# A third gathered tree, normalised rows and row sums kept in PSUM, and new orders in a fused attention and tree feed-forward kernel

## The reference

```python
x = x + attn(layernorm(x)); x = x + ffn(layernorm(x))
# attn: query, keys, values = unit_projection(x @ W.T + b)   f = fft(y); y = ifft(f/(|f|+1e-8)).real
#       s = cumsum(bind(keys, values), axis=1); out = unbind(s, query)        (products of spectra)
# ffn:  8 trees of depth 7 with 255 nodes each. logits = x @ W_in.T + b_in; decisions = logits > 0
#       a token walks from the root of each tree to one leaf; acts = silu(logits) count only on the path
#       out = masked_acts @ W_out.T
```

## Time and profile before

| | us |
|---|---|
| median of 3 runs (1918.32 to 1920.07) | 1919.68 |
| profiled execution, device time | 1920.69 |
| its span, first to last instruction | 1918.9 |
| TensorE busy in it | 1867.1 |
| VectorE busy | 1500.1 |
| ScalarE busy | 1118.4 |
| GpSimd busy | 946.1 |

### The profile page before, as it was taken

The page is one execution under the profiler, slowest core; times in us unless marked ns, Lnnn a source line. Parts: engine busy times, 40 slices in busy tenths (PEclk is TensorE's granted clock), DMA queues, the critical chain, the costliest instruction groups (busy, mean ns, idle before and its releaser), DMA issues.

```text
span 1918.9 us, 40326 instructions
## 1 busy us (share of the span) xinstructions
PE 1867.1 (97%) x14680; PEld 1417.2 (74%) x14680; DVE 1500.1 (78%) x2874; ACT 1118.4 (58%) x2151; POOL 946.1 (49%) x736
## 2 busy tenths in 40 slices
PE   8599999999999999999999999999999999999978
PEld 6478777778777778877777877777877777887755
DVE  4878778877877877877877877787787787788783
ACT  5666565566555566556556656556656555655643
POOL 1254445564454565444555444556444556545450
PEclk9799999999999999999999999999999999999998
DMA  8022232222133222223222223222213322222212
GB/s 285 12 78 81 74 99 88 77 88 87 55 99 99 66 88 88 67 86 99 77 84 86 82 66 99 93 71 88 88 56 97 99 75 79 88 67 87 88 56 66
DMA packets 181784, 163.18 MB, mean 85 GB/s; under 512 B 140160, under 2 KB 140800, under 8 KB 181760
## 3 DMA queue, kind: packets, MB, share of 16 engines
q1 hardware_dynamic: 163328, 95.48, 16.8%
q0 software_dynamic: 18432, 67.38, 10.6%
HBM read 95.72 MB, written 16.78 MB: 59 GB/s over the span
## 4 chain that ended last, share of the span: by engine, by line
PE 93%; DVE 1%; DMA 0%; SPq 0%; ACT 0%; issue 0%; DVEq 0%; ACTq 0%
PE bank_l L531 31%; PE bank_l L591 30%; PE bank_p L481 24%; PE bank_l L541 3%; PE bank_i L481 2%; PE bank_i L552 1%; PE bank_i L561 0%; PE bank_i L562 0%; PE bank_i L560 0%; PE bank_i L559 0%; DMA arena<-xn_pair 0%; PE bank_i L558 0%; PE bank_i L571 0%; SPq L340 0%; DVE xn_pair L1127 0%
## 5 line engine op out<-in xcount | busy, mean ns | idle before, releaser
L531 PE MATMUL bank_l<-arena,win_mem 128*128 128x256 f16 x5376 | 626.1, 273 | 14.4 <-DMA arena<-xn_pair 14.4
L591 PE MATMUL bank_l<-wout_mem,arena 128*128 128x512 f16 x2688 | 590.6, 379 | 0.0
L531 PEld LDWEIGHTS bank_l<-arena,win_mem 128*128 128x128 f16 x5376 | 527.3, 99 | 76.5 <-DMA arena<-xn_pair 14.2
L481 PE MATMUL bank_p<-arena,wf_hi 128*128 128x256 f16 x3072 | 506.3, 273 | 2.7 <-ACT arena L742 2.7
L591 PEld LDWEIGHTS bank_l<-wout_mem,arena 128*128 128x128 f16 x2688 | 263.1, 98 | 303.4 <-DVE arena L1224 0.2
L481 PE MATMUL bank_p<-arena,wf_lo 128*128 128x256 f16 x1536 | 419.3, 273 | 0.0
L986 POOL TENSOR_TENSOR arena<-arena 128x512 f32<-128x512 f32 x96 | 121.7, 1268 | 570.2 <-ACT arena L751 570.2
L481 PEld LDWEIGHTS bank_p<-arena,wf_hi 128*128 128x128 f16 x3072 | 299.8, 98 | 37.7 <-ACT arena L742 3.0
L796 ACT ACTIVATE arena<-bank_l,bias_in,s_logit 128x256 f32<-128x256 f32 x448 | 229.6, 556 | 142.1 <-PE bank_l L541 141.6
L1224 DVE SCALAR_TENSOR_TENSOR arena<-arena,s_act 128x512 f16<-128x512 f32 (+1 forms) x256 | 195.5, 765 | 133.7 <-ACT arena L806 131.2
L1217 DVE TENSOR_SCALAR dec<-bank_l,thr,off 128x256 bf16<-128x256 f32 x256 | 135.8, 541 | 91.5 <-PE bank_l L531 88.8
(11 more groups left out here) (178 smaller groups left out, 2490.3 us busy)
## 6 DMA issues: line engine op xcount, KB each, us to landing
arena<-in_x SPq DMA_DIRECT2D x32, 512.0 KB, 3.5
arena<-arena SPq DMA_DIRECT2D x32, 512.0 KB, 2.9
out<-arena SPq DMA_DIRECT2D x64, 256.0 KB, 2.1
wout_mem<-in_w_in_t SPq DMA_DIRECT2D x1, 3584.0 KB, 15.4
arena<-in_w_out_t SPq DMA_DIRECT2D x1, 3584.0 KB, 14.2
arena<-xn_pair SPq DMA_TRANSPOSE x128, 2.7
arena<-in_leaf_rows,leaf_row POOLq DMA_INDIRECT x128, 5.5
win_mem<-in_wq SPq DMA_DIRECT2D x1, 1024.0 KB, 8.2
```

The lines of the kernel that those rows point to most:

```text
L481: mm = pe.matmul(bank, a, b, start=(n == 0), stop=(n == len(pairs) - 1))
L531: mm = pe.matmul(bank_l[t % 4][:, c * T:(c + 1) * T], a[:, k, w:w + P], x2t[:, :, b, k, :], start=(c == 0 and k == 0 and m == 0), stop=((t ...
L591: mm = pe.matmul(bank_l[j][:, :], a[:, m, tok], w[:, m, :], start=(m == 0 and a is a_hi and w is wout_hi), stop=(m == DENSE - 1 and a is a ...
```

## The change

1. Tree 2 is gathered too: 13 dense columns, three leaf fetches, dots, silus and adds a block.
2. `acts` is gone, and `HELD` = 4 is the ring of the decisions alone. `silu` writes its result back into the PSUM bank of its tree, and `act_high` and `act_low` read it there. A bank is free for tree t+4 only when `act_low` of tree t has run.
3. The normalised rows `xn2` lie in `bank_i`. `keep_row` (ScalarE) copies them to SBUF for the leaf dots.
4. Leaf rows are summed in PSUM: `begin_total` (ScalarE) copies `x1` to `bank_l[2]` and `bank_l[3]`, two `leaf_add` accumulate there, the third writes `y`. Adds and `result` of block i now stand in step i+1 of VectorE.
5. The Nyquist column's running sums are two products of 3 columns in place of five of 1 column.
6. The projections go in the order K, V, Q, and the orders of all engines are rewritten. `WARM` = 30 small products stand at the start of TensorE. The splitting of `w_out` moves into step 0, and the peak search for its scale behind V's projection in step 0.
7. `down(i, 1)` is written in two parts, trees 0 to 5 and 6 to 7, ahead of `transform_back`.

```diff
-GATHERED = (0, 1)
+GATHERED = (0, 1, 2)
...
-ROUNDS = ((0, 1),)
+ROUNDS = ((0, 1, 2),)
...
-HELD = 3
+HELD = 4
...
-Q, K, V, G_IN, G_OUT = range(5)
+K, V, Q, G_IN, G_OUT = range(5)
...
+WARM = 30
...
-        xn2 = take(J * D).rearrange("p (j d) -> p j d", j=J)
+        kept = take(J * D).rearrange("p (j d) -> p j d", j=J)
...
-        acts = take(HELD * 2 * T).rearrange("p (r t) -> p r t", r=HELD)
...
-        y = fetched[:, 0, :, 0:D]
...
+        y = fetched[:, LEAVES - 1, :, 0:D]
...
-        sp_rows = bank_i[1][:, 0:3 * J].rearrange("p (j q) -> p j q", q=3)
-        sp_sums = bank_i[1][:, 8:8 + J + 1]
-        sp_size = bank_i[1][:, 16:16 + 3 * J].rearrange("p (j q) -> p j q", q=3)
+        xn2 = [bank_i[j][:, :] for j in range(J)]
+        total = [bank_l[2 + j][:, :] for j in range(J)]
+        sp_rows = bank_p[1][:, 0:3 * J].rearrange("p (j q) -> p j q", q=3)
+        sp_sums = bank_p[1][:, 8:8 + J + 1]
+        sp_size = bank_p[1][:, 16:16 + 3 * J].rearrange("p (j q) -> p j q", q=3)
...
-                    pe.wait_ge(act_ready, TREES * i + t - 3)
...
-                        pe.wait_ge(act_ready, TREES * (i - 1) + 5 + t)
+                        pe.wait_ge(leaf_added, LEAVES * i)
...
-                pe.matmul(sp_sums[:, 0:1], upper, sp_kv[:, 0:1], start=True, stop=True)
-                pe.matmul(sp_sums[:, 1:2], upper, sp_kv[:, 1:2], start=True, stop=False)
-                pe.matmul(sp_sums[:, 1:2], full, sp_kv[:, 0:1], start=False, stop=True)
-                pe.matmul(sp_sums[:, 2:3], full, sp_kv[:, 0:1], start=True, stop=False)
-                pe.matmul(sp_sums[:, 2:3], full, sp_kv[:, 1:2], start=False, stop=True).then_inc(sp_sums_full, 1)
+                pe.matmul(sp_sums[:, 0:3], upper, sp_kv[:, 0:3], start=True, stop=False)
+                pe.matmul(sp_sums[:, 0:3], full, sp_kv[:, 2:5], start=False, stop=True).then_inc(sp_sums_full, 1)
...
+            def down(i, j, trees):
...
-                if isinstance(i, int) and i == 0:
+                if isinstance(i, int) and i == 0 and trees[0] == 0:
...
-                pe.wait_ge(act_ready, TREES * i + 5 + j)
-                for t in range(TREES):
+                if trees[0] == 0:
+                    pe.wait_ge(a_lo_ready, TREES * i + 5 + j)
+                for t in trees:
...
                 pe.wait_ge(sp_carry_ready, n + 1)
-                for j in range(J):
-                    pe.wait_ge(x1_ready, J * i + j + 1)
+                pe.wait_ge(x2t_ready, 16 * J * (i + 1))
+                pe.wait_ge(xn2_kept, J * (i + 1))
+                for j in range(J):
...
                     project(n, K)
                     project(n, V)
+                if isinstance(i, int) and i == 0:
+                    peaks_in_row(G_OUT)
+                    peak_to_all(G_OUT)
+                if attn:
+                    project(n, Q)
                 logits(i, 0, 0)
                 logits(i, 1, 0)
+                if attn:
+                    nyquist_rows(n)
                 counts(i, 0)
                 logits(i, 2, 0)
-                logits(i, 2, 1)
                 logits(i, 3, 0)
+                counts(i, 1)
                 logits(i, 3, 1)
-                counts(i, 1)
+                counts(i, 2)
                 logits(i, 4, 0)
-                leaf_rows_of(i, 0)
-                if attn:
-                    nyquist_rows(n)
                 logits(i, 4, 1)
                 logits(i, 5, 0)
-                counts(i, 2)
+                counts(i, 3)
                 logits(i, 5, 1)
-                counts(i, 3)
+                counts(i, 4)
+                leaf_rows_of(i, 0)
                 logits(i, 6, 0)
+                counts(i, 5)
                 logits(i, 6, 1)
+                logits(i, 7, 0)
                 if attn:
                     nyquist_sums(n)
-                counts(i, 4)
-                counts(i, 5)
-                logits(i, 7, 0)
                 logits(i, 7, 1)
                 counts(i, 6)
-                down(i, 0)
-                down(i, 1)
+                down(i, 0, range(TREES))
+                down(i, 1, range(0, 6))
+                down(i, 1, range(6, TREES))
                 if attn:
                     transform_back(i)
...
+            def high2(n, j):
+                act.wait_ge(ln2_done, J * n + j + 1)
+                act.activation(xn_pair[:, j, 0, :], xn2[j], ACT.Copy).then_inc(xn2_hi_ready, 1)
+            def keep_row(n, j):
+                if not isinstance(n, int) or n:
+                    act.wait_ge(leaf_dot_ready, LEAVES * n)
+                act.wait_ge(xn2_lo_ready, J * n + j + 1)
+                act.activation(kept[:, j, :], xn2[j], ACT.Copy).then_inc(xn2_kept, 1)
+            def begin_total(i, j):
+                act.wait_ge(a_lo_ready, TREES * i + 7 + j)
+                act.activation(total[j], x1[:, j, :], ACT.Copy).then_inc(total_begun, 1)
...
-                if t >= HELD:
-                    act.wait_ge(a_lo_ready, TREES * i + t + 1 - HELD)
-                elif not isinstance(i, int) or i:
-                    act.wait_ge(a_lo_ready, TREES * i)
                 for c in [c for c in range(2) if (t, c) in COLUMN]:
-                    ins = act.activation(acts[:, t % HELD, c * T:(c + 1) * T], bank_l[t % 4][:, c * T:(c + 1) * T],
+                    ins = act.activation(bank_l[t % 4][:, c * T:(c + 1) * T], bank_l[t % 4][:, c * T:(c + 1) * T],
...
-                               acts[:, t % HELD, 0:wide * T].rearrange("p (c t) -> p c t", c=wide), ACT.Copy,
+                               bank_l[t % 4][:, 0:wide * T].rearrange("p (c t) -> p c t", c=wide), ACT.Copy,
...
                 if isinstance(i, int) and i == 0:
+                    for c in range(PIECES):
+                        wout_high(c)
...
+                    act.wait_ge(wout_lo_done, PIECES)
+                silu(i, 0)
...
                     add_eps(n, K)
+                    sum_squares(n, Q)
+                    add_eps(n, Q)
+                    bind(n)
                     q_unit(n)
-                    bind(n)
-                fetch(i, 1)
-                fetch(i, 0)
+                for g in range(LEAVES):
+                    fetch(i, g)
...
+            def normalise2(n):
+                dve.wait_ge(ln2_std, n + 1)
+                dve.reciprocal(rs2[:, :], rs2[:, :]).then_inc(ln2_rstd, 1)
+                dve.wait_ge(ln2_rstd, n + 1)
+                for j in range(J):
+                    dve.tensor_scalar(xn2[j], x1[:, j, :], mv2[:, j, 0:1], rs2[:, j:j + 1], ALU.subtract,
+                                      ALU.mult).then_inc(ln2_done, 1)
...
+            def low2(n):
+                for j in range(J):
+                    dve.wait_ge(xn2_hi_ready, J * n + j + 1)
+                    dve.tensor_tensor(xn_pair[:, j, 1, :], xn2[j], xn_pair[:, j, 0, :],
+                                      ALU.subtract).then_inc(xn2_lo_ready, 1)
...
+            def residual_of(n, j):
+                if not isinstance(n, int) or n:
+                    dve.wait_ge(total_begun, J * (n - 1) + j + 1)
+                dve.wait_ge(idft_full, J * n + j + 1)
+                dve.wait_ge(xr_ready, 16 * (n + 1))
+                residual(n, j)
...
-                for j in range(J):
-                    ins = dve.scalar_tensor_tensor(out=x1[:, j, :], in0=fetched[:, g, j, ROW_OUT:ROW_OUT + D],
-                                                   scalar=leaf_act[:, g, j:j + 1], in1=x1[:, j, :], op0=ALU.mult,
+                else:
+                    dve.wait_ge(total_begun, J * (i + 1))
+                for j in range(J):
+                    to = y[:, j, :] if g == LEAVES - 1 else total[j]
+                    ins = dve.scalar_tensor_tensor(out=to, in0=fetched[:, g, j, ROW_OUT:ROW_OUT + D],
+                                                   scalar=leaf_act[:, g, j:j + 1], in1=total[j], op0=ALU.mult,
                                                    op1=ALU.add)
...
+                first_z_low()
+                low(1, xn1, xn1_hi_ready, xn1_lo_ready)
+                win_low(2)
+                win_low(3)
+                dve.wait_ge(rows_summed, 3 + 2 * PIECES)
+                peak_of(G_OUT, PIECES)
+                peak_row(G_OUT)
                 scale_group(G_OUT)
                 feed_forward_constants()
-                first_z_low()
-                wout_low(0)
-                wout_low(1)
...
-                dve.wait_ge(x1_ready, J * i + J)
-                stats(i, x1, st2, mv2, ln2_stat, ln2_mv)
-                normalise(i, x1, xn2, mv2, rs2, ln2_std, ln2_rstd, ln2_done)
-                low(i, xn2, xn2_hi_ready, xn2_lo_ready)
+                begun = not isinstance(i, int) or i > 0
+                if begun:
+                    leaf_add(i - 1, 0)
+                residual_of(i, 0)
+                residual_of(i, 1)
+                stats2(i)
+                if begun:
+                    leaf_add(i - 1, 1)
+                normalise2(i)
+                low2(i)
+                if begun:
```

(36 more changed lines are left out.)

423 lines of the change are left out of this document (207 added, 216 removed).

## The result

| | before | after |
|---|---|---|
| median of the runs, us | 1919.86 (four runs, 1918.32 to 1920.07) | 1989.9 (four runs, 1985.46 to 1993.12) |
| ratio, 95% interval | 1 | 1.0364 [1.0351, 1.0377] |
| profiled execution, us | 1920.69 | 1993.12, span 1991.3 |

The account below looks back on a forecast made before the run. TensorE's own work was taken to set each block: head 166.3, 30 blocks of 54.0 (1620) and last block 57.4 give a span of 1843.7, plus 0.8: 1844 us. The range was 1826 to 1880.

Parts of the forecast that it names:

- TensorE's work in a block: Fewer logits, down and Nyquist products save 3.1 us: a block goes from 56.87 to 53.7 us if no wait is added.
- PSUM forms: Activations and normalisation written to PSUM and VectorE adds inside it: 0.1 us faster to 0.2 slower each.
- The bank reuse: Tree 4 waits for `act_low` of tree 0, which ends at 22.9 us for 23.4: in time by about 0.5.
- the four slacks: Waits at tree 4, tree 5, the inverse transform and the next block's transposes, with 0.4 to 0.8 us in hand each.
- Table loads: ScalarE has four in a block, 2.6 us more, without drain; the rival with a 1.38 us drain gave 1877, chance 0.04.
- The leaf fetches: Six take 7.9 us; two dots and tree 5's `act_low` behind the second end at 39.5, TensorE wants it at 40.1.
- The inverse transform and the next block's input: z ends at 51.7 us for 52.4, the next block's transposes land at 14.9 for 15.7: both in time.
- The head: First logits at 119.6 us, 8.7 lost in step 0 to splitting `w_out`, first block ends at 166.3, 13 later than before.
- Late banks or late z: Rival: two of the four waits miss and a block costs 55.2 us, 1880 in all; chance 0.25.
- In each other's way; slower than before: Rival: `act_low` and `leaf_add`, one input in PSUM, wait for GpSimd, up to 1.1 us each: 1935 us; chance 0.04.
- the lower bound of 157: End of the head's first block, in us, if the pieces of `w_out` hide under the late projections.

Follow-up runs that it names:

- e1: The kernel after with `unbind`'s four GpSimd products put between the pairs of fetches, nothing else changed; 1847.5 us, ratio 0.9622.
- e10: The kernel after with a memset of one column on GpSimd between the second and third of the six fetches; 1895.8 us, ratio 0.9873.
- e6: The kernel after with a memset of 192 columns on GpSimd between each two of the six fetches; 1853.2 us, ratio 0.9665.
- e14: The kernel of e10, word for word, run again in another set beside the kernel after; 1987.5 us, ratio 1.0359.
- e15: The kernel after, unaltered, run a third time to mark the condition of its set; 1985.7 us, ratio 1.0348.
- e7: e1's order with the `w_out` peak search ahead of block 1's projections and its splitting behind the first normalised rows; 1831.2 us, ratio 0.9553.
- e8: The kernel of e7 with `WARM = 0`, without the 30 warming products at its start; 1833.3 us, ratio 0.9557.
- e18: The kernel of e7, run again in another set beside the kernel after; 1835.7 us, ratio 0.9567.
- e5: The kernel after with fetches of 64 rows in place of 128 from block 1 on; 1898.5 us, ratio 0.9897.
- e9: The kernel after with a memset of 192 columns only between the second and third fetch; 1893.1 us, ratio 0.9848.
- e12: The kernel after with a memset of 192 columns only between the fourth and fifth fetch; 1900.7 us, ratio 0.9898.

## Why the prediction was wrong, by its own steps

The span was forecast as 1843.7 and is 1991.3, 147.6 more. The chain of waits places the ends, in its rows below: the first inverse transform at 177.60 (forecast 166.3, +11.3), the last at 1932.98, so 30 blocks of 58.51 (forecast 54.0, +135.4), and the last block 58.3 (forecast 57.4, +0.9).

```profile
177.60 15.72 PE bank_p L492 x144
...
1931.62 1.37 PE bank_i L492 x24
```

**TensorE's work in a block: right.** 53.7 was forecast, and e1 shows 53.80, with no wait. Cutting `down(i, 1)` in two moved nothing.

**PSUM forms: right.** The bounds were 0.1 faster to 0.2 slower. `act_low` out of PSUM at full width takes 0.74 us, the silu written back 0.53, and the adds in PSUM 0.70 each, as in the earlier trace rows. The first half-width `act_low` of the block, after:

```profile
959.37 0.48 DVE L1296 SCALAR_TENSOR_TENSOR arena<-bank_l,s_act,arena 128x256 f16<-128x256 f32 x1 [0.39 <-ACT arena L848]
```

It ends 23.2 us after the block's start, where 22.9 was worked out; TensorE did not wait there. The bank reuse, which looked like the tightest of the four slacks, held in every block.

**Table loads: right.** Four loads of 1.28 us a block, and the next instruction 0.01 later:

```profile
984.88 1.28 ACT L830 ACT_TABLE_LOAD   x1
986.17 0.48 ACT L830 ACTIVATE leaf_act<-leaf_dot,arena 128x1 f32<-128x1 f32 x2
```

The drain of 1.38 us that the Trainium skill (ScalarE: Activation LUTs, What ACT_TABLE_LOAD costs) puts on a switch would have shown here, and in e1's 53.80 us without a wait; it does not.

**The leaf fetches: this step failed, twice over.** It said: "Two dots, 1.3, and the `act_low` of tree 5, 0.7, queued behind them, end at 39.5; TensorE wants it at 40.1."

The first fault could have been seen in the rows. The landing was sized well (second fetch at 37.2 in e10, forecast 37.5). But with the fetches done, GpSimd goes straight into `unbind`, and the two dots, both inputs in SBUF, run into its two-input products. In e10 they take 2.45 and 1.74 us, from 1039.73 to 1043.79, instead of 1.3 in all; `act_low` ends near 42.0 for 40.1 wanted, and TensorE waits 1.82. GpSimd's timeline in e10 at that moment:

```profile
1040.35 1.27 POOL L1063 TENSOR_TENSOR arena<-arena 128x512 f32<-128x512 f32 x1
1041.70 1.60 POOL L1065 TENSOR_TENSOR arena<-arena 128x512 f32<-128x512 f32 x1
```

Each dot ends 0.56 us after one of these products (1041.62 and 1043.30). The effect was in the earlier trace rows, a dot of 1.63 us beside its sister of 0.68 (the row at 1050.81, which the prediction counts as a dot, is the subtraction of `low`, with two inputs in SBUF as well), and I used it against one-PSUM-input operations, where it does not act, and not in the sum for the two-SBUF-input dots. Its price over e10's span is one number:

```profile
PE bank_l L599 <- DVE arena L1299: 48.5, 30, 1.8
```

48.5 us. By the blocks it is 1.66 each: 28 blocks of e10 take 55.46 on average (172.31 to 1725.08), against 53.80 in e1. The medians differ by 48.3, which is so near in part by chance, as head and last block differ too. Most of e10's blocks take 55.7; those in which the fetch lands early enough for the first dot to be done, in 0.69 us, before GpSimd's product starts take 54.03. e6 is the test of it: its fillers push `unbind` back, the dots fall beside fetches alone, and e6's block takes 53.7 in most cases, with 6.2 us of waiting for `act_low` in all. A fetch does not stretch them:

```profile
1019.11 0.69 DVE L1313 SCALAR_TENSOR_TENSOR arena<-arena 128x512 f32<-128x512 f32 x1 [0.98 <-DMA arena<-in_leaf_rows,leaf_row]
...
1019.22 1.40 POOL L1113 DMA_INDIRECT arena<-in_leaf_rows,leaf_row  x1 [0.17 <-issue]
```

The Trainium skill (SBUF — State Buffer, SBUF: two separate sides) says that only a VectorE operation with two SBUF inputs, or in a two-port mode, meets GpSimd on a shared port; the traces agree on both counts: `act_low` out of PSUM keeps its 0.74 us beside a product of GpSimd's, in e10 as below, and the dots do not.

```profile
1043.79 0.74 DVE L1299 SCALAR_TENSOR_TENSOR arena<-bank_l,s_act,arena 128x512 f16<-128x512 f32 x1
...
1043.38 1.59 POOL L1067 TENSOR_TENSOR arena<-arena 128x512 f32<-128x512 f32 x1
```

The second fault is the late signals. No term stood for them, and nothing in the trace of before shows one. Their price is e14 against e10, one program: the medians are 91.7 us apart (1987.5 and 1895.8), the spans of the two profiled runs 88.3 (1982.7 and 1894.4), 2.9 a block. Of that 1.9 is waiting: e14's waits for the test and the `act_low`, without the 8.4 of the head, are 81.0 - 8.4 + 32.6 = 105.2 us, against 48.5 in e10, 56.7 more.

```profile
PE bank_l L554 <- DVE dec L1292: 81.0, 31, 8.4
PE bank_l L599 <- DVE arena L1299: 32.6, 28, 2.6
```

Another 1.0 is clock: TensorE's busy time is 1807.7 us in e14 and 1777.4 in e10, 30.3 more for the same products, 24.3 of it in the down products. Together 87.0 of the 88.3. The pages of both, e10's first:

```profile
PE 1777.4 (94%) x14036; PEld 1336.2 (71%) x14036; DVE 1565.2 (83%) x3130; ACT 1253.4 (66%) x2403; POOL 939.8 (50%) x833
```

```profile
PE 1807.7 (91%) x14036; PEld 1342.4 (68%) x14036; DVE 1489.9 (75%) x3130; ACT 1253.3 (63%) x2403; POOL 924.3 (47%) x833
```

So the 4.5 us too many in a block are -0.2 (53.8 for 54.0), +1.7 for the dots and +2.9 for late signals. They overlap in the trace: VectorE is busy 76 us less in the kernel after than in e10, 51 of them in the dots (182.1 for 233.0), which I read as dots that the late test has moved off GpSimd's products. With prompt signals the kernel after should take about 1895 us, by e10, 1.3% faster than before and still outside the range; it was not measured so.

**The inverse transform and the next block's input: right.** In e1, where TensorE never stalls in the loop, neither `z` nor the transposes were late, though both had under a microsecond in hand.

**The head: right in mechanism, 6 to 11 us short.** The wait for the test of tree 1 in step 0 was forecast as 8.7 and is 8.4. In e15 block 1's projections start at 92.25, forecast 92.3; e15's head ends at 172.25, 6.0 late. VectorE's residual starts at 107.1 for 105.7, the first logits at 123.2 for 119.6, and 2.4 of the 6.0 come in step 0, where 0.7 is a wait for `act_low` and, behind the wait for the test, 12 logit products take 2.77 us in place of 1.47. What delays the first logits is a wait not foreseen, Q's projection for V's bank; it lasts 9.9 us, and 2.2 of it is not covered by the chain that was counted. ScalarE empties that bank (L774) only behind `std(0)`, which waits for the residual. e15's ScalarE and TensorE:

```profile
114.45 0.29 ACT L716 ACTIVATE rs<-mv,ln_eps 128x2 f32<-128x2 f32 x1 [12.67 <-DVE mv L1144]
114.65 0.82 ACT L774 ACTIVATE arena<-bank_p,bias_f 128x256 f32<-128x256 f32 x2
115.53 0.60 PE L492 MATMUL bank_p<-arena,wf_hi 128*128 128x256 f16 x2 [9.89 <-ACT arena L774]
```

In the profiled run of the kernel after the head ends another 5.4 us later. There the clock is 0.53 between 20 and 30 us, with TensorE busy throughout, and 0.79 in the next 10; in e15 it is 1.00 in both, and block 1's projections start 8.5 us earlier. After, then e15:

```profile
20.00:30.00 10.00, 10.00 (x27) 0.53 1.06 281
```

```profile
20.00:30.00 10.00, 10.00 (x44) 1.00 1.04 269
```

With or without the 30 first products (e7, e8) single runs scatter by 6 to 9 us, so that was no cure. e7 takes back 15 of the head's microseconds with its two moves together; what each gives was not run. Its 157.09 meets the lower bound of 157 by luck, as that bound had only the pieces of `w_out` moved.

**The rivals.** "Late banks or late z" was the nearest: a late `act_low` of tree 5, but by the dots and not by banks or z. "In each other's way; slower than before" had the right pair of engines and the wrong operations. A cause outside this list decided the sign. What stays open: by which path a row of fetches holds up TensorE's signals, and what sets the condition. It was there in five of eight sets and not in the other three, with and without on one chip; with the bytes halved it stayed. Each trace is one run of its set, and the timed runs beside it agree with it.

## What to carry to other kernels

A row of four to six indirect fetches issued by GpSimd back to back can delay the signals of TensorE; put other GpSimd work between the pairs (e1 and e18; a filler of one column was not enough), and count no slack near such a row as safe. When two-input products of GpSimd move, lay VectorE's operations with two SBUF inputs against them again, at 1.7 to 2.5 us in place of 0.7. And before a small edit is said to cure something, run the uncured kernel beside it in the same set: six experiments here seemed to cure it (e5, e6 and e9 to e12); one of them, e10, run again, did not, and the other five were not run again.

## What was not expected of the hardware

- TensorE's signals reached ScalarE and VectorE 3.9 us late while six indirect fetches were issued 1.25 us apart, in five of eight sets of runs, and some 1 us late with four in the one such set that had them; one program took 1895.8 or 1987.5 us by it.
- VectorE's dots of two SBUF inputs kept 0.69 us beside an indirect fetch of GpSimd's (e6) and took 1.7 to 2.5 us where they met its two-input products (e10).
- After a wait of 2.5 us TensorE ran a stretch of 2 us at a granted clock of 0.50, and the engine's busy time grew by 30 us over the span.
- TensorE, busy throughout, was granted 0.53 from 20 to 30 us in one run and 1.00 in another of the same kernel.
